# One core, four layers fused: attention steps that begin after four heads' maxima, with the later batches' queries computed between them in a PSUM bank of their own

## The reference, cut to what matters

```
x = x + gelu_tanh(layernorm(x) @ ctx.T) @ ctx                    # per batch
x = x + gate * (gelu(layernorm(x) @ W1[e]) @ W2[e])              # 8 experts, capacity routing
q = layernorm(x) @ Wq.T;  k = ctx @ Wk.T;  v = ctx @ Wv.T        # 16 heads of 16
x = x + softmax(q k.T + bias(relative position), masked) v @ Wo.T
x = x + 0.3 * ((gelu(x @ w1[sel] + b1) @ w2[sel] + b2) @ Wo + bo)    # expert sel chosen per batch
```

## Time and profile before

| | us |
|---|---|
| median of 3 runs | 706.75 (706.34 to 709.12) |
| the profiled execution, its own time | 713.54 |
| its span, first to last instruction | 711.3 |
| expert pairs end on PE | 372.8 |
| first max product | 381.9 |
| first scores, step 0 | 423.5 |
| step 5 | 439.6 |
| step 16 (batch 1 begins) | 476.7 |
| last steps end | about 628 |

### The profile page before, as it was taken

The page is one execution under the profiler, slowest core; times in us unless marked ns, Lnnn a source line. Parts: engine busy times, 40 slices in busy tenths (PEclk is TensorE's granted clock), DMA queues, the critical chain, the costliest instruction groups (busy, mean ns, idle before and its releaser), DMA issues.

```text
span 711.3 us, 8691 instructions
## 1 busy us (share of the span) xinstructions
PE 650.4 (91%) x3030; PEld 369.9 (52%) x3034; DVE 320.4 (45%) x936; ACT 276.3 (39%) x388; POOL 67.6 (10%) x67
## 2 busy tenths in 40 slices
PE   3999999999998868899994789999999999999997
PEld 1666666666666545566762333334344444345443
DVE  4334333003006672122624848887887876213100
ACT  1111111111112331332230676666686687863321
POOL 0000000000002002344410000000020020022000
PEclk9999999999998997999997799999999999999999
DMA  9992302403001121611207330204204000300510
GB/s 322 385 352 74 119 0 97 156 0 126 0 1 47 55 74 49 195 60 66 91 22 198 96 99 2 67 17 130 79 16 121 1 3 7 114 1 0 171 38 29
DMA packets 48436, 61.94 MB, mean 87 GB/s; under 512 B 8644, under 2 KB 41638, under 8 KB 47974
## 3 DMA queue, kind: packets, MB, share of 16 engines
q1 hardware_dynamic: 46054, 55.91, 24.5%
q0 software_dynamic: 2336, 5.45, 2.3%
HBM read 43.64 MB, written 11.09 MB: 77 GB/s over the span
## 4 chain that ended last, share of the span: by engine, by line
PE 79%; DVE 11%; ACT 3%; issue 3%; DMA 2%; SPq 1%; DVEq 0%; POOL 0%; POOLq 0%; ACTq 0%
PE ps L541 13%; PE ps L552 13%; PE ps L1029 7%; PE ps L1016 6%; PE ps L981 6%; PE ps L753 5%; PE ps L725 4%; PE ps L832 4%; PE ps L840 4%; DVE arena L1904 3%; PE ps L699 2%; PE ps L850 2%; PE ps L802 2%; PE ps L788 2%; PE ps L620 1%
## 5 line engine op out<-in xcount | busy, mean ns | idle before, releaser
L1904 DVE TENSOR_REDUCE arena<-ps 128x1 f32<-128x416 f32 x256 | 137.6, 583 | 38.2 <-PE ps L981 37.3
L1367 ACT ACTIVATE arena<-ps 104x1024 f32<-104x1024 f32 x128 | 124.6, 1022 | 50.6 <-PE ps L1016 50.6
L541 PE MATMUL ps<-xnT,arena 128*128 128x512 f32 x208 | 101.8, 615 | 0.9 <-DVE xnT L1466 0.9
L552 PE MATMUL ps<-arena 128*128 128x256 f32 x416 | 100.0, 385 | 0.0
L1169 ACT ACTIVATE arena<-ps 128x512 f32<-128x512 f32 x52 | 31.0, 597 | 175.9 <-PE ps L541 175.9
L552 PEld LDWEIGHTS ps<-arena 128*128 128x128 f32 x416 | 80.8, 194 | 33.7 <-issue 24.9
L981 PE MATMUL ps<-arena 97*128 97x416 bf16 x256 | 78.5, 347 | 6.5 <-DVE arena L1904 3.9
L1016 PE MATMUL ps<-arena 100*104 100x512 bf16 x256 | 76.0, 381 | 1.6 <-ACT arena L1218 0.8
L1029 PE MATMUL ps<-arena 104*32 104x512 f32 x512 | 68.2, 604 | 0.7 <-ACT arena L1367 0.7
L981 PEld LDWEIGHTS ps<-arena 97*128 97x128 bf16 x256 | 21.0, 97 | 74.7 <-issue 42.1
L1466 DVE COPY xnT<-ps 128x512 f32<-128x512 f32 x16 | 10.4, 687 | 101.0 <-PE ps L514 101.0
(11 more groups left out here) (222 smaller groups left out, 695.9 us busy)
## 6 DMA issues: line engine op xcount, KB each, us to landing
arena<-in_W SPq DMA_DIRECT2D x16, 512.0 KB, 8.8
arena<-in_ctxT SPq DMA_DIRECT2D x4, 1664.0 KB, 7.7
arena<-in_ctxN SPq DMA_DIRECT2D x4, 1664.0 KB, 12.5
arena<-arena SPq DMA_DIRECT2D x48, 128.0 KB, 2.4
arena<-last_k_parts SPq DMA_DIRECT2D x48, 104.0 KB
last_k_parts<-arena SPq DMA_DIRECT2D x24, 104.0 KB, 1.8
x_tok<-in_x SPq DMA_DIRECT2D x4, 512.0 KB, 9.0
xn_rows<-xn SPq DMA_DIRECT2D x4, 512.0 KB, 5.4
```

What stands on the lines that cost most here:

```text
L541: ins = pe.matmul(ps[:, 4 + k % 2, :], ctxT_s[:, b % 2, c, f * P:f * P + P], xnT[:, c, S * b:S * b + S], start=(c == 0), stop=(c == KC - 1))
L552: ins = pe.matmul(ps[:, b % 2 * 2 + t // 2, t % 2 * D:t % 2 * D + D], hid[:, (k - 2) % 4, t * P:t * P + P], ctxN_s[:, b % 2, f, :], start= ...
L1367: act.activation(pexp2[0:KT, u % 4, :, :], ps[0:KT, 2 + 2 * (u % 2):4 + 2 * (u % 2), :], ACT.Exp).then_inc(f_pe, 1)
L1904: dve.tensor_reduce(cmax2[:, h, j:j + 1], ps[:, banks.place(key), 0:KF], AX.X, ALU.max).then_inc(banks.is_taken(key), 1)
```

## The change

1. The prelude holds only max products, `ahead(0)` = 24 of them, each followed by one `keep_busy` product; 12 such products stand ahead (9 before) and 5 behind. DVE reduces 20 maxima before it adds any answer. The first group's transpose comes 2 maxima after the group's end, not 4.
2. The queries of batches 1 to 3 are computed in steps 2 to 16 of batch 0 (`QUERY_NORM`, `QUERY_TURN`, `QUERY_START`). From step 4 to step 17 one of the three rotating banks is set aside for their products, so that all else rotates over two.
3. DVE's remaining work (layer norm of batch 1, answers and norms of batches 2 and 3) is dealt out beside the maxima, one or two pieces after each.
4. The first part's rows of batch 0 (6 DMAs) go out on ACT's queue, the answers of batches 1 to 3 on POOL's; SP keeps the other 6 and then loads keys of batch 1 earlier. ACT computes one exponential of a zero in the prelude.
5. In the routing stage the last key-and-value product stands ahead of the two waits of PE for the token marks instead of behind them, and 11 `keep_busy` products follow instead of 5.

```diff
+GROUP_TAKE = {end + (AFTER if i else AFTER // 2): i for end, i in GROUP_END.items()}
 X_TURN, X_PROJECT, X_NORM, X_ROWS, X_ROUTE, X_LOGITS = (3, 4), (5, 7), (11, 12, 12, 13), (13, 14), 1, 3
 ROUTES = ((0, 2), (2, B))
 
 QUERY_BANKS = ((6, 7), (4, 5), (2, 3), (4, 5))
+QUERY_START = {4: (1, 0), 6: (1, 1), 8: (2, 0), 10: (2, 1), 12: (3, 0), 14: (3, 1)}
+QUERY_TURN = {2: (1, 0), 3: (1, 1), 6: (2, 0), 7: (2, 1), 10: (3, 0), 11: (3, 1)}
+QUERY_NORM = {1: (1, 0), 2: (1, 2), 5: (2, 0), 6: (2, 2), 8: (3, 0), 9: (3, 2)}
+OWN, OWN_FROM, OWN_UPTO = 2, 4, 17
...
-    return min(B * AU + AFTER + 1, 28 + 5 * st, 44 + 4 * st)
+    return min(B * AU + AFTER + 1, 24 + 5 * st + max(0, (st - 8) // 2), 44 + 4 * st)
...
+        i = self.active[self.turn % len(self.active)]
+        self.turn += 1
+        if self.uses[i]:
+            pe.wait_ge(self.taken[i], self.uses[i])
+        self.uses[i] += 1
+        self.at[key] = (i, self.uses[i])
+        return self.banks[i]
...
+    def set_aside(self, i):
+        self.active = [j for j in self.active if j != i]
+
+    def take_back(self, i):
+        self.active = sorted(self.active + [i])
...
+            last_product(LAST - 1)
...
-            last_product(LAST - 1)
             pe.wait_ge(s_ekp, KC * B)
             pe.wait_ge(s_ev, 2 * B)
-            keep_busy(5)
+            keep_busy(11)
...
+                        if m in GROUP_TAKE:
+                            turn_maxima(GROUP_TAKE[m])
                         if m < AU * B:
                             max_product(m)
+                        keep_busy(fillers, 6)
...
+                    if k == 0:
+                        pe.wait_ge(s_qp, KC * b + m)
+                        if b == 1 and m == 0:
+                            pe.wait_ge(banks.taken[OWN], banks.uses[OWN])
+                    query_product(b, m, k, own_bank)
+
+                keep_busy(12)
                 pe.wait_ge(s_qp, KC)
-                max_products(FIRST)
-                turn_queries(1, 0)
-                turn_queries(1, 1)
-                max_products(FIRST + 2)
-                product(1, 0, 0)
-                product(1, 0, 1)
-                max_products(FIRST + 3)
-                product(1, 1, 0)
-                product(1, 1, 1)
-                query_rest(1, 0, 0)
...
-                query_rest(3, 0, 1)
-                query_rest(3, 1, 0)
-                max_products(ahead(0))
-                query_rest(3, 1, 1)
-                pe.wait_ge(s_qp, KC * B)
+                max_products(ahead(0), 1)
+                keep_busy(5, 6)
...
+                    if st == OWN_FROM:
+                        banks.set_aside(OWN)
+                    if st == OWN_UPTO:
+                        pe.wait_ge(s_qp, KC * B)
+                        banks.take_back(OWN)
                     for hp in range(HG // 2):
                         scores(st, hp)
                         max_products(ahead(st) + hp + 1)
+                        if st in QUERY_START:
+                            product(*QUERY_START[st], hp)
+                        if hp == 0 and st - 1 in QUERY_START:
+                            bi, m = QUERY_START[st - 1]
+                            query_rest(bi, 0, m, own_bank)
                     if t == 2 and st >= CT:
                         turn_values(st // CT - 1)
+                    if b == 0:
+                        max_products(ahead(st) + 3)
...
+                    if st - 1 in QUERY_START:
+                        bi, m = QUERY_START[st - 1]
+                        query_rest(bi, 1, m, own_bank)
+                    if st in QUERY_TURN:
+                        turn_queries(*QUERY_TURN[st])
...
+                act.wait_ge(s_q1, KC)
+                for half in range(2):
+                    for r in range(TERMS):
+                        if Q_PARTS[r] == 0:
+                            act.dma_start(Q2[r:KR:TERMS, 0, half * HH:half * HH + HH, :], query_part_at(0, 0, half)).then_inc(f_rows[0][half], 16)
+
+                act.wait_ge(s_zt, 1)
+                act.activation(one_t[:, :], zero_t[:, 0:1], ACT.Exp)
...
+                    if st - 2 in QUERY_START:
+                        bi, m = QUERY_START[st - 2]
+                        query_part(bi, 2, m, own_bank)
...
+                def first_norm():
+                    if piece[0] < norm_pieces(1):
+                        norm_piece(1, 1, piece[0])
                         piece[0] += 1
-                        if piece[0] == norm_pieces(2) - 3 * 2:
+
+                def add_answers_of(k):
+                    b, t = 2 + k // TB, 2 * TB + k
+                    if k % TB == 0:
+                        dve.wait_ge(s_gat[b], 16)
+                    ins = dve.scalar_tensor_tensor(x_tok[:, t, :], yg[:, t, :], gate[:, t:t + 1], x_tok[:, t, :], ALU.mult, ALU.add)
+                    if k % TB == TB - 1:
+                        ins.then_inc(s_moe, 1)
+
+                def last_norms():
+                    k = late[0] - 2 * TB
+                    if late[0] < 2 * TB:
+                        add_answers_of(late[0])
+                    elif k < norm_pieces(2):
+                        if k == 0:
+                            dve.wait_ge(s_moe, B)
+                        norm_piece(2, 2, k)
+                        if k == norm_pieces(2) - 1:
                             dve.sem_inc(s_lnst, 1)
+                    late[0] += 1
+
+                def beside_first_batch():
+                    if piece[0] < norm_pieces(1):
+                        first_norm()
+                        first_norm()
+                    else:
+                        last_norms()
+                        if late[0] > 2 * TB + 3 * 2:
+                            last_norms()
...
-                max_steps(FIRST)
+                max_steps(TB * GROUPS[0][2] + AFTER)
                 add_answers(1)
                 dve.wait_ge(s_moe, 2)
-                for k in range(norm_pieces(1)):
-                    norm_piece(1, 1, k)
...
+                max_steps(ahead(0), beside_first_batch)
...
-                load_answers()
                 sp.wait_ge(f_ones[0], 16)
                 for half in range(2):
                     sp.wait_ge(f_keys[0][half], 16 * KEY_LOADS)
@@ -2216,6 +2233,8 @@
 
                     i, hs = b % 2, slice(half * HH, half * HH + HH)
                     for part, s_part in enumerate((s_q1, s_q2, s_qp)):
+                        if b == 0 and part == 0:
+                            continue
                         sp.wait_ge(s_part, KC * b + half + 1)
                         for r in range(TERMS):
                             if Q_PARTS[r] == part:
@@ -2231,17 +2250,17 @@
 
                 query_ones(0)
                 queries(0, 0)
-                load_answers()
                 queries(0, 1)
-                query_ones(1)
-                for half in range(2):
-                    queries(1, half)
                 for half in range(2):
                     sp.wait_ge(f_rows[0][half], 16 * TERMS)
+                sp.wait_ge(s_ysd, first_pairs + (LAST_PAIRS + 1))
                 for half in range(2):
                     keys(1, half)
                 key_ones(1)
+                query_ones(1)
                 router_weights()
+                for half in range(2):
+                    queries(1, half)
...
+            for i in range(2):
+                pool.wait_ge(s_evst[i], 16)
+            for b in range(1, B):
+                pool.dma_start(yg[:, TB * b:TB * b + TB, :], yt_d[S * b:S * b + S, :].rearrange("(t p) d -> p t d", p=P)).then_inc(s_gat[b], 16)```

The order of PE's instructions shows what this does at three places. Names in the rows: `bank_takenN` counts how often the rotating bank N was read out; `q_parts_made` counts third parts of queries.

In the routing stage, PE before (L681 are the products with the token marks, L620 the last key-and-value product, L626 `keep_busy`):

```order
L599 MATMUL ps<-arena,minus_eye_b 128x416 [waits last_k_second_part]
L681 MATMUL ps<-arena 128x56 [waits slots_marked,router_exp_then_own_index]
L681 MATMUL ps<-arena 128x56 x7
L681 MATMUL ps<-arena 128x56 [waits slots_marked]
L681 MATMUL ps<-arena 128x56 x7
L620 MATMUL ps<-wv,arena 104x256 [waits last_keys_loaded3,last_k_parts_made]
L620 MATMUL ps<-wv,arena 104x256 x3
L626 MATMUL ps<-cst 128x256 [waits last_v_taken,last_k_parts_made]
L626 MATMUL ps<-cst 128x256 x4
```

169 lines of the change are left out of this document (59 added, 110 removed).

## The result

| kernel | median, us | runs |
|---|---|---|
| before | 707.93 | 706.34 to 710.86, 4 runs |
| changed | 722.49 | 721.37 to 723.4, 4 runs |

The changed kernel is **slower** by 2.0%: ratio 1.020, 95% interval 1.016 to 1.0241. It lies outside the range of the prediction, 709.0 (701.0 to 715.0). The changed kernel's profiled execution took 722.88 us, with a span of 721.0. All ratios in this document leave out the few runs that lie far above the others of their kernel, and are taken within one set of runs, so that they are not always the quotient of two medians.

A forecast was written before the change was run, and what follows sets the result against it. The prelude was taken as a chain, the steps as bound by PE. Routing -2.0, prelude with steps 0 to 4 -14.1, queries +13.7 and two banks +4.7 gave +2.3 on 706.75: 709.0 us, range 701.0 to 715.0.

The forecast's parts named there:

- The start of the maxima: Before the first max product: PE reaches it at 382.2, 0.3 us later than before; the two queues buy nothing.
- Routing: Routing stage: moved product and eleven fillers let the transposes start earlier, -2.0 us, ends -3.2 and +0.8.
- Prelude: From first max product to step 0: step 0 starts at 401 instead of 423.5, -22.5 us.
- Steps 0 to 4: First five steps: DVE binds with work moved from the prelude; they take 24.5 us, before 16.1.
- Steps 5 to 15: Eleven later steps: PE binds with a bank less; 37.1 us before, plus 13.7 of products and 4.7 of waits.
- queries: Steps 5 to 15, on PE: added query products, subtractions, turns and four more max products, +13.7 us.
- two banks: Steps 5 to 15: waits added by rotating over two banks instead of three, +4.7 us, ends 0 and +8.
- The price of one late product: With two banks, the third product in a row waits 1.03 - 0.36 = 0.67 us.
- The count by hand: Steps 5 to 15: bank waits followed through the order step for step, 8.2 us against some 2.7 before.
- Rival (b): Steps 0 to 4: PE's clock drops, +4 us, and later waits +6.5; sum +8.1, time 715, chance 0.28.

The follow-up runs named there:

- e4: The changed kernel with the second half's rows issued only once the first half's landed, and the answers only after all twelve row transfers: 713.77 us, ratio 1.0065.
- e8: The kernel before with the routing edit alone (last product moved ahead, eleven fillers): 709.68 us, ratio 1.0004.
- e1: The changed kernel with POOL's queue loading the answers only after all twelve row transfers of batch 0 have landed: 715.4 us, ratio 1.0101.
- e3: The changed kernel with batch 0's rows and the answers transferred as before, all on SP, answers between the halves: 714.77 us, ratio 1.0103.
- e12: e4 without DVE's eight adds of the answers of batches 2 and 3 (output lacks them): 711.92 us, ratio 1.0035.
- e5: The kernel before with one of three score banks set aside, empty, in steps 4 to 17, queries staying in the prelude: 714.82 us, ratio 1.0079.
- e15: e13 without the filler products between the prelude's max products: 712.73 us, ratio 1.0068.
- e13: e4 with one max product of steps 1 to 16 moved ahead of the use of the values: 714.88 us, ratio 1.0107.
- e6: The changed kernel without the filler products between the prelude's max products: 720.31 us, ratio 1.0145.
- e14: The kernel before with one max product moved ahead of the use of the values in all steps: 703.99 us, ratio 0.9939.

## Why the prediction was wrong, point by point

- **The start of the maxima: the step that failed.** "So the two queues buy nothing here: whatever they bring forward, PE reaches the first max product at 382.2." That the queues bring no gain was right: even in e4, with the queues undisturbed, PE comes to the product when its `keep_busy` end. But the step priced the moved transfers by their issue alone, and so took their cost as nothing. The change also took the answers from behind the first half's rows and the second half's from behind the answers, and started all of them beside the 0.75 MB that PE's first product needs, 3.0 MB together. Expected +0.3 us, measured +7.6; that is 7.3 of the 11.8 us between the forecast's sum (+2.3) and the sum of the parts (+14.1). The sentence of the Trainium skill on shared engines was read for what a second queue can save, not for what it can cost, and no rival had this case.
- **Routing -2.0**: nothing (e8). The term came from one execution's clock. The trace was known to be 6.8 us over the median shown, and the term rested on a half clock in it.
- **Prelude**: 18.8 us forecast, 20.0 measured, since after 7.3 us of waiting PE ran the first max products and fillers at half clock (one filler in 1.06 us instead of 0.60; the clock is 0.92 on average in the window). With the wait gone, e1 and e3 have 18.5 at a clock of 1.00.
- **Steps 0 to 4**: DVE binds, 24.5 us forecast and 24.1 measured: right, and e12 shows the cause.
- **Steps 5 to 15**: queries +13.7, measured 14.2; two banks +4.7, measured +6.0 in e5. The price of one late product, 0.67, was right (1.03 - 0.36 us, as in e5). The count by hand gave 8.2 of waits less before's 2.7, so 5.5; what was taken off it for waits that serve two reasons made it worse. The mechanism was right, the size short by 1.8 in all.
- **Rival (b)**, a lower clock in steps 0 to 4, came true: the clock was 0.86 on average in these steps, at 0.50 from 416 to 420, behind PE's waits for DVE. But it cost far less than the 4 us that the rival gave it: 0.7 us by the changed kernel's 24.1 against e15's 23.4, 1.2 by e13's 24.6 (also 0.86), from which e15 differs by the fillers alone. The rival's 715 rested on a reason that did not decide.
- Without the start's loss, the change would still be slower than before, e4 by 0.65% (interval 0.33 to 0.97%). A prelude of 19 us instead of 41.6 saves 22.6; DVE's work that left it costs 7.7 in steps 0 to 4, the queries 14.2 in steps that had no room on PE, the missing bank 6.0. Together that is 5.3 us more than before, by the parts.

Left open: whether the fillers cost anything beyond their 1.2 us of prelude (e6's total is not clear enough to say), and whether the short wait read off e14's rows is all that its order takes away.

## What to carry to other kernels

When a transfer moves to another queue, list everything that is then on its way together with the transfer that is waited for, and divide the bytes by the rate that the trace shows (here 3.0 MB at 240 GB/s, some 12 us). Give the engines to the waited one by holding the rest back on its semaphore (here 7 to 9 us). Work that moves from a stretch of idle engines into one where an engine is full costs its full length there, and also what the buffer that it takes along is worth: count both before the gain at its old place. A term that only one execution shows, above all one with the clock in it, needs a second profile. A short wait can stand in the profile as busy time: compare the starts of the same products in two kernels, not only the waits that are listed.

## What the runs showed of the hardware

- Four products in 32-column tiles run side by side: all four in 1.07 us, two of them in 1.05 us, and one other product between them makes two groups of it (+46 us in 64 steps). The Trainium skill (TensorE: Matmul & The Clock Gate, "Part 3: Packing small matmuls — row/col tiling") says that such tiles overlap; these rows agree.
- The same 128 KB transfers on ACT's queue landed in 3.4 us (median of six, e4) with one half's rows under way, and in 8.1 us (changed kernel) with the other half's and 1.5 MB of answers beside them.
- A bank came back 1.03 us after its max product began. With two banks instead of three the third product in a row came 0.67 us late (e5), 6.0 us in eleven steps.
